# A MetaFormer block on one core: the last quarter of the convolution in two parts, the gate's chunks between their steps, five row buffers in place of three

## The chip, the cores and the metric

The kernel runs on one NeuronCore of a Trainium2 chip. Its engines are TensorE (PE in the profile, with PEld for its weight loads), VectorE (DVE), ScalarE (ACT) and GpSimd (POOL); SyncE (SP) issues nearly all plain DMAs, and GpSimd issues the indirect ones. The engines run their own instruction streams and wait for one another through semaphores. The metric is the device time of one execution, in microseconds.

## The reference, cut to what matters

`x` is 16 images of 64 channels and 56 x 56 pixels, in float32. Two blocks are computed, one after the other:

```
v = ln_over_channels(x)
r = relu(batchnorm(w1 @ v + b1))                    # 16 channels
ker = w2 @ r + b2                                   # 7 x 7 taps for each of 16 groups, at each pixel
x = x + sum over taps of shifted v * ker            # "involution": 16 groups of 4 channels
t = tokens of x (50176 of 64)
g = ln(t) @ Wg + bg;  top 2 of 8 experts, softmax over the two
t = t + sum over the two experts of weight * (gelu(ln(t) @ W1 + b1) @ W2 + b2)
```

All of it is kept to float32 accuracy.

## The kernel before, in words

Four stages follow one another, with a barrier of all engines between two: `norm_stage`, `conv_gate_stage`, `expert_stage`, `merge_stage`. The change lies in `conv_gate_stage`, and in `pieces` (line 693), which says where the pixels of a chunk lie in the images and which all later stages use.

**The convolution.** The images are taken in two parities of 8 images, and the rows of an image in two halves of 28. That gives four quarters (`QUARTERS`, line 79), and each quarter has a step for each of the 16 groups: 64 steps `t`. A step works on three strips of rows (`STRIP_SETS`, line 78). The first strip holds two blocks of 7 output rows, the other two strips one block each. For a strip, SP loads `xq` (112 or 119 partitions of 8 KB, lines 880 and 883), and once a step a `band` of filter weights (line 867). The first strip of a step, and the band, are split into a high and a low part: ACT writes the high parts (`split_band` line 959, `split_maps` line 965), DVE subtracts for the low ones (`low_parts`, line 1124). PE then needs three fast matmuls per product for that strip (lines 1054 to 1056). The other two strips are multiplied in plain float32 (line 1060), where one matmul is two instructions in the profile.

The products come in 8 units a step (`UNITS_OF`, line 86), 2 products of 119 x 448 each: units 0 to 3 for the split strip, 4 and 5, 6 and 7 for the others. Each goes to one of three PSUM buffers `z_ps`. DVE multiplies a unit by the reduced maps `r_all` (`weigh`, line 1135) into `prod`, and PE adds the blocks' taps up into `o_ps` (`sums`, line 1063). The sums of strips 0 and 1 stand after units 5 and 7 of the same step; those of strip 2 stand after unit 1 of the next step. Then ACT copies `o_ps` to `ob` (`evacuate`, line 979, first in ACT's work of a step) and SP stores it in eight DMAs (`store`, line 886).

**The order on each engine** is written out by hand. In step `t`, SP loads band and maps of `t`, then stores step `t-2`, then loads a chunk (lines 920 to 931); `store` waits for the evacuation, and all loads behind it in the queue wait with it. ACT evacuates `t-1`, splits band and maps of `t+1`, then does its share of the gate (line 1015). DVE does `low_parts(t+1)` after unit 3. PE's first unit of a step waits for both low parts (line 1039).

**The gate.** The 50176 tokens are 56 chunks of 896, 14 a quarter; a chunk can be worked on when its quarter's convolution has been stored. `load_chunk` (line 908) brings x and the convolution for it, in two DMAs for each image the chunk touches. PE's `unit` (line 1079) makes the centred rows and the raw gate scores, ACT takes them out of `u_ps` (`take_unit`, line 984), DVE adds up the squares (`variance`). Two chunks are a batch. ACT's `deviation` and DVE's `scores`, `first_choice`, `second_choice`, `number_duo` rank a batch in one step ("the rank step"); in the next ("the place step") DVE scans the batch, PE counts over the partitions (`counts`, line 1093), DVE fills the rows (`fill_rows`) and finds their places (`places`), and then POOL scatters the batch's rows to DRAM in 14 indirect DMAs (line 950). Rows and indices have three buffers (`RR`, line 711). `step_of` (line 845) puts chunk `c` of a quarter beside step `c + 2` of the next quarter. The last quarter has no next one: its 14 chunks are run in steps 66 to 79, with no convolution beside them.

After the last batch DVE works out a table of tiles (lines 1297 to 1364), SP stores it and writes 28 blank tiles at addresses that it reads from SBUF (line 938), and the stage ends when all of this and POOL's rows have landed.

**Later stages.** In `expert_stage` SP also loads x and the convolution chunk by chunk (`load_base`, line 1447); in `merge_stage` it stores each pair of chunks, one DMA for each image that a chunk touches (line 1679).

## Time and profile before

| | us |
|---|---|
| median of 3 runs | 2650.18 (2648.71 to 2662.69) |
| the profiled execution | 2656.94 |
| its span, first to last instruction | 2655.0 |
| granted TensorE clock, mean | 0.868 |
| PE busy, 10208 matmuls | 2018.9 (76%) |
| DVE busy | 1501.6 (57%) |
| ACT busy | 851.4 (32%) |
| POOL busy | 932.1 (35%) |

A busy share is an average over stages: PE is at 8 or 9 tenths in the slices of the convolution and of the experts, and at 3 to 1 tenths in three slices in the middle. Of POOL's time, 407.6 us are the 392 indirect DMAs of the gate, each 1040 ns.

### The profile page before, as it was taken

The numbers are of one execution on the slowest core, as the hardware profiler recorded it, in microseconds if no ns is written. First come the engines' busy times: TensorE is split into PE (matmuls) and PEld (weight loads), VectorE is DVE, ScalarE is ACT, GpSimd is POOL, SyncE is SP. The second block draws the span as 40 slices with busy tenths as digits, with TensorE's granted clock in tenths as the row PEclk, the third lists the DMA queues.
The fourth block names the chain that finished last, engine by engine and source line by source line (L and its number), as shares of the span: only waits on it lengthen the run. The fifth ranks groups of instructions, "written<-read, shape, count | busy, mean of one in ns | idle before, by whom it ended". The sixth has DMA issues, their size and how long they took to land. (4 is left out here: it accounts for less than half of the span.)

```text
span 2655.0 us, 34527 instructions
## 1 busy us (share of the span) xinstructions
PE 2018.9 (76%) x10208; PEld 1217.5 (46%) x10208; DVE 1501.6 (57%) x2687; ACT 851.4 (32%) x1540; POOL 932.1 (35%) x977
## 2 busy tenths in 40 slices
PE   5975889989889989898888321388787778778845
PEld 3742444445454445454444321255455555445533
DVE  2433566658778678786777534145444444444423
ACT  2431111122231222222322211255455555555510
POOL 5000000002433232430442566156555555555520
PEclk9977999999899999899999555689889899998965
DMA  8677777777877777777774320576666676766548
GB/s 238 143 155 172 181 190 188 184 188 204 203 187 186 194 193 194 195 180 199 195 202 102 86 63 32 153 211 199 188 198 197 195 199 196 200 191 201 165 123 274
DMA packets 291480, 474.17 MB, mean 179 GB/s; under 512 B 120156, under 2 KB 196059, under 8 KB 268327
## 3 DMA queue, kind: packets, MB, share of 16 engines
q1 hardware_dynamic: 260071, 441.41, 62.4%
q0 software_dynamic: 28832, 30.65, 4.1%
q8 instruction: 79, 1.29, 0.2%
q14 instruction: 98, 0.80, 0.1%
q10 hardware_dynamic: 2400, 0.01, 0.1%
HBM read 392.67 MB, written 81.93 MB: 179 GB/s over the span
## 5 line engine op out<-in xcount | busy, mean ns | idle before, releaser
L950 POOL DMA_INDIRECT token_rows<-gate_rows,gate_index x392 | 407.6, 1040 | 1039.1 <-DVE gate_index L1263 926.3
L1475 POOL DMA_INDIRECT mixed<-exp_mix,exp_xt x474 | 483.0, 1019 | 415.8 <-DVE exp_mix L1613 276.4
L1143 DVE TENSOR_TENSOR prod<-z_ps,r_all 119x896 f32<-119x896 f32 x512 | 543.2, 1084 | 130.3 <-PE z_ps L1056 79.5
L1060 PE MATMUL z_ps<-xq,band 112*119 112x448 f32 x1024 | 462.6, 588 | 123.3 <-DVE prod L1143 62.9
L1542 PE MATMUL exp_h_ps<-exp_tok,exp_pack 128*128 128x384 f32 x1264 | 292.2, 377 | 133.1 <-DVE exp_tok L1592 111.8
L1498 ACT ACTIVATE exp_hid<-exp_h_ps,exp_pack 128x384 f32<-128x384 f32 x632 | 341.3, 578 | 113.2 <-remote 67.1
L1060 PEld LDWEIGHTS z_ps<-xq,band 112*119 112x119 f32 x1024 | 185.9, 192 | 343.0 <-issue 259.6
L1542 PEld LDWEIGHTS exp_h_ps<-exp_tok,exp_pack 128*128 128x128 f32 x1264 | 234.2, 205 | 236.7 <-DVE exp_tok L1592 148.1
L1592 DVE CAST exp_tok<-exp_x_ps 128x384 fp32r<-128x384 f32 x158 | 88.1, 558 | 370.5 <-remote 216.8
L1554 PE MATMUL exp_y_ps<-exp_hid,exp_pack 128*64 128x384 f32 x1264 | 258.0, 532 | 0.0
L1073 PE MATMUL o_ps<-prod,pick 119*32 119x448 f32 x2048 | 254.2, 592 | 0.7 <-DVE prod L1143 0.3
L982 ACT ACTIVATE ob<-o_ps 128x448 f32<-128x448 f32 x64 | 34.8, 544 | 623.8 <-PE o_ps L1073 597.7
L1054 PE MATMUL z_ps<-xq_hi,band_hi 119*119 119x448 f32 x512 | 204.5, 399 | 25.9 <-DVE xq_lo L1132 18.0
L1055 PE MATMUL z_ps<-xq_lo,band_hi 119*119 119x448 f32 x512 | 187.6, 366 | 0.5 <-issue 0.5
L1056 PE MATMUL z_ps<-xq_hi,band_lo 119*119 119x448 f32 x512 | 187.2, 366 | 0.0
L1132 DVE TENSOR_TENSOR xq_lo<-xq,xq_hi 119x2048 fp32r<-119x2048 f32 x64 | 146.5, 2289 | 70.3 <-ACT xq_hi L970 69.1
L1505 ACT ACTIVATE exp_ysb<-exp_y_ps,exp_pack 64x384 f32<-64x384 f32 x158 | 90.9, 575 | 281.2 <-remote 135.2
L1088 PE MATMUL u_ps<-moe_gate_rhs,gate_xc 128*128 128x72 f32 x784 | 115.8, 309 | 73.8 <-issue 71.7
L970 ACT ACTIVATE xq_hi<-xq 119x2048 fp32r<-119x2048 f32 x64 | 122.2, 1909 | 137.7 <-DMA xq<-xs 132.1
L1054 PEld LDWEIGHTS z_ps<-xq_hi,band_hi 119*119 119x119 f32 x512 | 92.9, 182 | 133.3 <-issue 113.1
L1088 PEld LDWEIGHTS u_ps<-moe_gate_rhs,gate_xc 128*128 128x128 f32 x784 | 115.1, 226 | 77.3 <-issue 75.8
L1527 PE MATMUL exp_x_ps<-ident,exp_pair 128*128 128x128 f32 x474 | 88.0, 300 | 73.0 <-DVE exp_pair L1585 73.0
(194 smaller groups left out, 2119.6 us busy)
## 6 DMA issues: line engine op xcount, KB each, us to landing
xq<-xs SPq DMA_DIRECT2D x192, 896.0 KB
exp_pack<-packs SPq DMA_DIRECT2D x316, 321.5 KB
exp_xt<-token_rows SPq DMA_DIRECT2D x158, 120.0 KB
xs<-xpad SPq DMA_DIRECT2D x32, 448.0 KB, 5.7
xin<-in_x_dram SPq DMA_DIRECT2D x8, 1568.0 KB, 11.2
co<-ob SPq DMA_DIRECT2D x512, 24.5 KB
merge_yt<-mixed SPq DMA_DIRECT2D x28, 448.0 KB, 4.9
mixed<-exp_mix,exp_xt POOLq DMA_INDIRECT x474
```

Of the source, the lines that this page charges most:

```text
L950: pool.indirect_dma_start(out=token_rows[:, :], out_offset=bass.IndirectOffsetOnAxis(ap=index[b % RR][:, j:j + 1], axis=0), in_=rows[b % R ...
L1054: nc.tensor.matmul(zt, hi, maps[0], start=True, stop=False)
L1055: nc.tensor.matmul(zt, hi, maps[1], start=False, stop=False)
L1056: mm = nc.tensor.matmul(zt, lo, maps[0], start=False, stop=True)
L1060: mm = nc.tensor.matmul(zt, band[t % BR][rows_in, at:at + MF], maps, start=True, stop=True)
L1073: mm = nc.tensor.matmul(o_ps[32 * q:32 * (q + 1), 0:CN], pick[:, cols], prod[(NU * t + u) % PR][:, lot, :], start=i == 0 and lot == 0, sto ...
L1088: mm = nc.tensor.matmul(u_ps[:, GATE_COLS * j:GATE_COLS * (j + 1)], xc[n % XC][:, P * j:P * (j + 1)], tab.gate_rhs[:, :], start=True, stop ...
L1143: nc.vector.tensor_tensor(prod[(NU * t + u) % PR][:, :, :].rearrange("p m (d x) -> p m d x", d=D), z_ps[(NU * t + u) % 3][0:MF, :, 0:CN].r ...
L1475: pool.indirect_dma_start(out=mixed[:, :], out_offset=bass.IndirectOffsetOnAxis(ap=xt[t % XT][:, j, ROW_ID:ROW_ID + 1].bitcast(U32), axis= ...
L1498: nc.scalar.activation(hid[n % 8][:, :], h_ps[n % HT][:, 0:N], ACT.Gelu, bias=pack[t % WT][:, e, PACK_B1 + blk:PACK_B1 + blk + 1]).then_in ...
L1542: mm = nc.tensor.matmul(h_ps[n % HT][:, 0:N], pack[t % WT][:, e, cols].bitcast(F32R), tok[t % 2][:, :], start=not last, stop=last)
L1554: mm = nc.tensor.matmul(y_ps[t % 2][C * e:C * (e + 1), 0:N], pack[t % WT][:, e, at:at + C], hid[(t * 4 + BLK * e + blk) % 8][:, :], start= ...
```

## The change

- The last quarter (odd images, rows 28 to 55) is now two parts. The first is rows 42 to 55 of those images: 16 steps with the split strip alone. The second is rows 28 to 41: 16 steps with the two unsplit strips alone. The stage has 80 steps, the last 32 with 4 units each and 14 rows of output.
- Each of the two parts has 7 chunks, of 896 tokens as before; an image now gives 784 tokens to a part, so that every one of these 14 chunks touches two images.
- The chunks of the third quarter are put beside every second step of the first part (7 of them, steps 50 to 62), and beside the first 7 steps of the second part (64 to 70). The chunks of the first part are put beside the next 7 steps (71 to 77). Those of the second part stand behind the convolution (82 to 88).
- In the last 16 steps nothing is split: ACT and DVE have no high and low parts to make, and PE waits for the loads themselves.
- A loop of 8 slots remains in PE and DVE; a step of 4 units uses every second slot. The sums of a strip follow after the second unit that comes behind it.
- `RR` is 5 in place of 3.

The core of the diff:

```diff
-STRIP_SETS = ((0, 1, 2), (5, 4, 3))
-QUARTERS = ((0, 0), (0, 1), (1, 0), (1, 1))
+PARTS = ((0, 28, 0, (0, 1, 2)), (0, 28, 1, (0, 1, 2)), (28, 28, 0, (5, 4, 3)),
+         (42, 14, 1, (5,)), (28, 14, 1, (4, 3)))
+PART_CHUNKS = [height * W * P8 // CHUNK for _, height, _, _ in PARTS]
+CHUNK_STEPS = ([G + 2 + c for c in range(14)], [2 * G + 2 + c for c in range(14)],
+               [3 * G + 2 + 2 * c for c in range(7)] + [4 * G + c for c in range(7)],
+               [4 * G + 7 + c for c in range(7)], [5 * G + 2 + c for c in range(7)])
...
-    XR, PR, BR, XC, SQ, RR = 8, 6, 3, 3, 2, 3
+    XR, PR, BR, XC, SQ, RR = 8, 6, 3, 3, 2, 5
...
         def step_of(n):
-            return G * (n // QUARTER_CHUNKS + 1) + 2 + n % QUARTER_CHUNKS
+            k, c = part_of(n)
+            return CHUNK_STEPS[k][c]
...
+        SLOTS = len(UNITS_OF[0])
+        def unit_at(t, u):
+            if t >= STEPS:
+                return None
+            each = SLOTS // len(UNITS_OF[t // G])
+            return unit_no[t, u // each] if u % each == 0 else None
...
-                if t + 1 < STEPS:
+                if t + 1 < SPLIT_STEPS:
                     split_band(t + 1)
                     split_maps(t + 1)
...
-                if u == 0:
+                if split and u == 0:
                     pe.wait_ge(b_lo, t + 1)
                     pe.wait_ge(x_lo, t + 1)
-                elif u == LAST_UNIT[0] + 1 or u == LAST_UNIT[1] + 1:
-                    pe.wait_ge(x_in[n % XR], raw_uses(n % XR, n))
+                elif not split and (u == 0 or UNITS_OF[t // G][u - 1][0] != i):
+                    pe.wait_ge(band_in[t % BR], (t // BR + 1) * 16)
+                    pe.wait_ge(x_in[n % XR], raw_uses(n))
...
             for t in range(LAST):
-                for u in range(NU):
-                    if t < STEPS:
-                        filters(t, u)
-                    if u == 1 and 1 <= t <= STEPS:
-                        sums(t - 1, 2)
+                for u in range(SLOTS):
+                    v = unit_at(t, u)
+                    if v is not None:
+                        filters(v)
+                        for at in sums_after.get(v, ()):
+                            sums(*at)
                     if u == 2 and t in chunk_at:
                         unit(chunk_at[t])
-                    if u == 5 and t < STEPS:
-                        sums(t, 0)
                     if u == 6 and t in place_at:
                         counts(place_at[t])
-                    if u == 7 and t < STEPS:
-                        sums(t, 1)
...
-                    if u == 3 and t + 1 < STEPS:
+                    if u == 3 and t + 1 < SPLIT_STEPS:
                         low_parts(t + 1)
```

## Rows read from the trace of the kernel before

**Rows 1.** Stretches: length, busy per engine (instructions), granted clock, DMA share, GB/s.
```profile
1143.64:1455.95 312.31, 278.16 (x1364) 149.70 (x1364) 239.57 (x415) 77.09 (x117) 103.89 (x98) 0.95 0.68 177
1455.95:1655.90 199.95, 53.64 (x228) 50.30 (x228) 92.81 (x329) 40.48 (x75) 125.14 (x126) 0.51 0.21 61
```

**Rows 2.** Timeline of ACT, two steps: start, duration, line, operation, [idle before].
```profile
1377.35 0.55 ACT L982 ACTIVATE ob<-o_ps 128x448 f32<-128x448 f32 x1 [12.88 <-PE o_ps L1073]
...
1379.42 1.91 ACT L970 ACTIVATE xq_hi<-xq 119x2048 fp32r<-119x2048 f32 x1 [1.24 <-DMA xq<-xs]
1381.35 1.28 ACT L1003 ACT_TABLE_LOAD   x1
1382.64 0.31 ACT L1003 ACTIVATE gate_std<-gate_var,gate_eps_t 128x14 f32<-128x14 f32 x1
...
1402.42 0.55 ACT L982 ACTIVATE ob<-o_ps 128x448 f32<-128x448 f32 x1 [8.87 <-PE o_ps L1073]
...
1403.16 1.90 ACT L970 ACTIVATE xq_hi<-xq 119x2048 fp32r<-119x2048 f32 x1
...
1419.31 0.54 ACT L982 ACTIVATE ob<-o_ps 128x448 f32<-128x448 f32 x1 [12.89 <-PE o_ps L1073]
```

**Rows 3.** Timeline of ACT, the last evacuation of the convolution.
```profile
1455.94 0.54 ACT L982 ACTIVATE ob<-o_ps 128x448 f32<-128x448 f32 x1 [10.64 <-PE o_ps L1073]
```

**Rows 4.** Timeline of DVE in the same two steps.
```profile
1384.07 2.09 DVE L1143 TENSOR_TENSOR prod<-z_ps,r_all 119x896 f32<-119x896 f32 x2
...
1407.91 2.29 DVE L1132 TENSOR_TENSOR xq_lo<-xq,xq_hi 119x2048 fp32r<-119x2048 f32 x1
...
1411.11 0.17 DVE L1233 SCALAR_TENSOR_TENSOR gate_lean<-gate_side,gate_tanh 128x14 f32<-128x14 f32 x1
...
1412.42 2.08 DVE L1143 TENSOR_TENSOR prod<-z_ps,r_all 119x896 f32<-119x896 f32 x2
```

**Rows 5.** Groups by line, last quarter: busy, mean ns, idle before.
```profile
L1143 DVE TENSOR_TENSOR prod<-z_ps,r_all 119x896 f32<-119x896 f32 x128 | 135.5, 1083 | 23.5 <-PE z_ps L1060 7.4 <-PE z_ps L1056 6.7 <-remote 6.0
```

**Rows 6.** Timeline of PE in the same two steps.
```profile
1377.21 0.46 PE L1054 MATMUL z_ps<-xq_hi,band_hi 119*119 119x448 f32 x1
...
1378.52 1.68 PE L1088 MATMUL u_ps<-moe_gate_rhs,gate_xc 128*128 128x72 f32 x14
...
1406.39 3.17 PE L1060 MATMUL z_ps<-xq,band 112*119 112x448 f32 x8
1409.49 1.73 PE L1073 MATMUL o_ps<-prod,pick 119*32 119x448 f32 x16
```

**Rows 7.** Timeline of PE, a restart after an idle stretch.
```profile
905.08 1.67 PE L1060 MATMUL z_ps<-xq,band 112*119 112x448 f32 x4
911.34 3.34 PE L1060 MATMUL z_ps<-xq,band 112*119 112x448 f32 x4 [4.58 <-DVE prod L1143]
```

**Rows 8.** Timeline of SP's queue, one step: stores, chunk, band, maps.
```profile
1361.07 3.39 SPq L893 DMA_DIRECT2D co<-ob  x8
1364.50 0.51 SPq L916 DMA_DIRECT2D gate_xc<-in_x_dram  x1
...
1367.03 0.67 SPq L867 DMA_DIRECT2D band<-vf  x1
1367.75 1.01 SPq L880 DMA_DIRECT2D xq<-xs  x1
```

**Rows 9.** Timeline of PE behind the convolution, four of its chunks.
```profile
1466.63 3.23 PE L1088 MATMUL u_ps<-moe_gate_rhs,gate_xc 128*128 128x72 f32 x14 [0.65 <-issue]
...
1497.38 3.23 PE L1088 MATMUL u_ps<-moe_gate_rhs,gate_xc 128*128 128x72 f32 x14 [19.24 <-issue]
1501.84 3.24 PE L1088 MATMUL u_ps<-moe_gate_rhs,gate_xc 128*128 128x72 f32 x14 [1.22 <-issue]
...
1520.21 3.24 PE L1088 MATMUL u_ps<-moe_gate_rhs,gate_xc 128*128 128x72 f32 x14 [1.42 <-issue]
```

**Rows 10.** Timeline of POOL behind the convolution, single scatters [idle before].
```profile
1510.79 1.02 POOL L950 DMA_INDIRECT token_rows<-gate_rows,gate_index  x1 [17.32 <-DVE gate_index L1263]
...
1546.55 0.97 POOL L950 DMA_INDIRECT token_rows<-gate_rows,gate_index  x1 [0.31 <-issue]
1556.02 1.02 POOL L950 DMA_INDIRECT token_rows<-gate_rows,gate_index  x1 [8.50 <-DVE gate_index L1263]
```

**Rows 11.** Timeline of ACT behind the convolution, one chunk taken.
```profile
1540.01 0.54 ACT L990 ACTIVATE gate_rows<-u_ps 128x448 f32<-128x448 f32 x1 [20.14 <-issue]
```

**Rows 12.** Timeline of POOL and SP's queue, POOL's last scatter and the blank tiles.
```profile
1654.63 0.97 POOL L950 DMA_INDIRECT token_rows<-gate_rows,gate_index  x1 [0.30 <-issue]
...
1659.88 26.57 SPq L938 DMA_DIRECT2D token_rows<-moe_blank  x25
```

More of the change, by code:

```diff
@@ L88 @@
              for i, r in enumerate(strips) for q in range(0, CH, 3 - len(STRIP_BLOCKS[r]))]
-            for strips in STRIP_SETS]
-NU = len(UNITS_OF[0])
-LAST_UNIT = [max(u for u, (i, _) in enumerate(UNITS_OF[0]) if i == k) for k in range(len(STRIP_SETS[0]))]
+            for _, _, _, strips in PARTS]
 XS_H = C * P8 * WP
@@ L690, in _, with part_of @@
             dve.wait_ge(bn_own, 11)
+def part_of(n):
+    k = max(k for k in range(len(PARTS)) if FIRST_CHUNK[k] <= n)
+    return k, n - FIRST_CHUNK[k]
 def pieces(n):
-    quarter, c = divmod(n, QUARTER_CHUNKS)
-    s, par = QUARTERS[quarter]
+    k, c = part_of(n)
+    top, height, par, _ = PARTS[k]
+    per_image = height * W
     at, end = c * CHUNK, (c + 1) * CHUNK
@@ L699, in pieces @@
     while at < end:
-        i, pos = at // HALF, at % HALF
-        size = min(end - at, HALF - pos)
-        runs.append((PARITY * i + par, HALF * s + pos, at - c * CHUNK, size))
+        i, pos = at // per_image, at % per_image
+        size = min(end - at, per_image - pos)
+        runs.append((PARITY * i + par, top * W + pos, at - c * CHUNK, size))
         at += size
@@ L845, in step_of @@
         def step_of(n):
[L846 removed]
+            k, c = part_of(n)
+            return CHUNK_STEPS[k][c]
         def placing_step(b):
@@ L914, in load_chunk @@
                 for img, at, to, size in pieces(n):
-                    for lot, part in enumerate((x, co)):
+                    for lot, maps in enumerate((x, co)):
                         sp.dma_start(xc[n % XC][C * lot:C * (lot + 1), to:to + size],
-                                     part[img].rearrange("c h w -> c (h w)")[:, at:at + size]
+                                     maps[img].rearrange("c h w -> c (h w)")[:, at:at + size]
                                      ).then_inc(xc_in[n % XC], 16)
@@ L922, in _ @@
                     load_band(t)
-                    for i in range(GS):
+                    for i in range(len(part(t)[3])):
                         load_maps(t, i)
-                        for part in range(len(R_PARTS)):
-                            if R_STEPS[part] == t and i == min(part, 1):
-                                load_r(part)
+                        for lot in range(len(R_PARTS)):
+                            if R_STEPS[lot] == t and i == min(lot, 1):
+                                load_r(lot)
                 if 0 <= t - 2 < STEPS:
@@ L1063, in sums @@
             def sums(t, i):
-                pe.wait_ge(weighted, NU * t + LAST_UNIT[i] + 1)
+                last = len(part(t)[3]) - 1
+                blocks = [m for r in part(t)[3] for m in STRIP_BLOCKS[r]]
+                pe.wait_ge(weighted, strip_end[t, i])
                 if i == 0 and t >= 1:
                     pe.wait_ge(ob_done, t)
-                for u, (kind, parts) in enumerate(UNITS_OF[quarter_of(t)[0]]):
+                for u, (kind, parts) in enumerate(UNITS_OF[t // G]):
                     if kind != i:
@@ L1273, in _ @@
                 if t in R_NEED:
-                    dve.wait_ge(r_ready, max(part for part in range(len(R_PARTS)) if R_NEED[part] == t) + 1)
-                for u in range(NU):
-                    if t < STEPS:
-                        weigh(t, u)
+                    dve.wait_ge(r_ready, max(lot for lot in range(len(R_PARTS)) if R_NEED[lot] == t) + 1)
+                for u in range(SLOTS):
+                    if unit_at(t, u) is not None:
+                        weigh(unit_at(t, u))
                     if u == 1 and t in rank_at:
```

164 lines of the change are left out of this document (93 added, 71 removed).

## The prediction

> **What bounds the kernel now.** I read the page first: its 40 slices show PE at 8 or 9 tenths in the convolution and in the experts, and a trough between them. The stretches give it a size [rows 1]: the last quarter takes 312.3 us from the evacuation before it to the last one, with PE 89% and DVE 77% busy. Behind it lie 199.95 us until POOL's last scatter, with PE 27% busy at half clock and DMA at 0.21. This second stretch is what the change shortens, by running 7 of its 14 chunks beside the convolution. It can pay for that only in the first.
>
> Next the timeline of a pair of steps in the convolution [rows 2]. Evacuations stand at 1377.35, 1402.42 and 1419.31: a rank step of 25.1 us and a place step of 16.9 us, seven of each in a quarter. The place step is full: the reader can add PE's work [rows 6], where four split units are 4 x 1.31, the other two strips 2 x 3.17, the sums 2 x 1.7 and the chunk 1.5: 16.5 us. The rank step is long because DVE waits for the deviation, which ACT makes only after it has split the next step's maps, here 1.24 us late for their DMA. PE then runs dry, and a restart shows what that costs beyond the wait [rows 7]: the same four instructions take 1.67 us before 4.58 us of idle time and 3.34 after it. That is TensorE at 1.2 GHz where it had been at 2.4.
>
> Last the tail. A chunk that meets no obstacle follows the one before after 4.46 us, 1497.38 to 1501.84 [rows 9]. But POOL needs about 18 us for a batch: 14 scatters of 0.97 us with 0.30 between them are 17.8, and two batches back to back took 36.7, 1510.79 to 1547.5 [rows 10]. While it works off two batches the other engines slow down: PE begins the chunk at 1520.21, 3.24 us of work by its records, and ACT gets it at 1540.01 [rows 9, 11]. SP writes only 3 of its 28 blank tiles until POOL has stopped, then 25 in 26.6 us [rows 12]. I do not know why; that it goes with POOL's runs is what the rows show.
>
> **The first part: 16 steps with the split strip alone.** The work would fit into 7 us: PE has 4 x 1.31 + 1.7 = 6.9 us, DVE four products and the low parts, 4 x 1.05 + 2.6 = 6.8 [rows 4 to 6]. What sets the step is a chain that a long step hides behind its other strips. From the evacuation of t-1: ACT's copy, band and maps, 2.64 us (1402.42 to 1405.06); DVE's low part, 2.29; PE's first two units of t+1, 2.62, and the sums of t, 1.73, which release the next evacuation. With hand-overs that is 9.35 us [rows 2, 4, 6]. PE is then idle at least 2.4 us a step, so part of it runs at 1.2 GHz; nothing gives +0, all of PE's share twice as long gives +4.35. I take +2, since the slow stretch is one of a few us [rows 7]. That makes 11.3 us.
>
> The loads are a second chain. The maps of t+1 stand in SP's queue behind the store of t-2, which waits for an evacuation, and on even steps behind a chunk. The maps are issued 6.7 us after the stores begin with a chunk and 4.2 without [rows 8]. They landed 11.7 us later at the latest (1367.75 to 1379.42), with three strips a step in the queues; here there is one, and I take 6.5. So on even steps the split can begin 0.6 + 6.7 + 6.5 = 13.8 us after the evacuation one step earlier, and two steps take 13.8 + 8.6 + 2 = 24.4 us. Seven such pairs are 171 us, two steps without chunks 22.6. Three rank steps add 1.6 for table and deviation, 1.1 for the scores and a product ahead of the low parts, 3.9 each; three place steps add `fill_rows`, 1.3 to 1.5 [rows 2, 4]. The sum is 210 us. Its ends are 166 (the bare chain) and 235 (all at 1.2 GHz, no more DMA waits).
>
> **The second part: 16 steps with the two unsplit strips.** PE has 6.3 + 1.7 + 1.5 + 0.2 = 9.7 us where there is a chunk [rows 6]. DVE has 4.2 for the products; the gate costs it (239.57 - 135.5 - 15 x 2.7) / 14 = 4.5 us a chunk, together 8.8 [rows 1, 4, 5]. The DMA engines are busy 0.68 of 19.5 us now [rows 1]; with two strips of three, half the stores and a chunk a step I estimate 9.5 to 10. Three resources near 10 us do not interlock without loss. The rank step no longer waits for a split, so I take 11.4 for 14 steps and 18.6 for the two without a chunk: 178 us, between 153 and 216. SP has 3.4 + 2.5 + 0.7 + 1.7 = 8.3 us of issuing a step, which fits, though it is close.
>
> The quarter thus goes from 312.3 to 388 us, **+76**; both parts at their ends would give +7 and +139.
>
> **The tail.** Before, POOL's last row begins 198.7 us after the last evacuation, at 1654.63, and ends at 1655.6: E + 199.7 [rows 3, 12]. After it: the first chunk at E + 10.7 as now (1455.94 to 1466.63), the third 2 x 4.46 later; it stands in the step that places batch 24, and POOL starts 8.95 us after such a chunk (1501.84 to 1510.79), at E + 28.6. Two batches and the idle time behind them take 45.2 us (1510.79 to 1556.02), since the chunks stall as now; the last two batches, at 18.1 each between the two figures above, end at E + 28.6 + 45.2 + 36.2 = E + 110. **-90**. Without idle time between batches it is E + 101 (-99); with the 17.3 us of idle time before one batch [rows 10], and one more such gap, -73. What follows POOL's last row, mostly the 25 blank tiles, stays.
>
> **At nothing.** Five row buffers: when ACT took the chunk at 1540.01, POOL's batch in that slot, the first of the pair, had ended at about 1528.9, so three did not hold it. I cost them at 0, with up to -9 if the idle time of 8.5 us were theirs. Two more memsets lie ahead of the first loads' landing: 0 to 2 us. Chunks that touch two images bring 8 more DMAs in each loop: in the experts SP has room, in the merge stage up to 0.6 each; I take +1, bounds 0 and +6.
>
> Sum: 76 - 90 + 1 = -13, with rounding -14. The profiled execution, 2656.9 us, would be 2643; it lies 6.8 above the median of the runs, so the median comes to **2636 us**.
>
> **Rivals.** (1) *TensorE stays at 1.2 GHz all through the first part.* For it: every step leaves PE idle behind its burst, and the clock has fallen after such a gap [rows 7]. Then a step without chunk takes 5.0 + 8.7 = 13.7 us; with one, PE's own work of 3 + 5.2 delays it to about 16: with the 16 us for rank and place steps that is 9 x 13.7 + 7 x 16 + 16 = 251 us, 41 more than my 210: 2677 us, slower. It decides once PE's share of the chain runs at half clock in every step, and not only in its first units. Against it: gaps in the trace are followed by only a few slow us. The Trainium skill, "TensorE: Matmul & The Clock Gate", section "HAM oscillation — how this bites in real kernels", states this rule: where each burst is shorter than the wait before it, every burst starts cold. The trace agrees for one burst [rows 7]; by that rule the sum is this rival's, by the short slow stretch it is mine.
>
> (2) *The chains overlap better.* Maps land sooner and the clock holds: first part 185, second 170, and the tail's batches follow without idle time: 43 - 99 + 1 = -55, 2595 us. For it: the DMA queues have a third of the strips. Against it: the chain of 9.35 us is in the order of the program.
>
> (3) *POOL's runs meet.* In the second part a batch is due every 22.8 us and takes 18. If DVE places one late and the next early, PE stalls as at 1520.21, 16.6 us a time (1523.4 to 1540.0). Two such stalls are +33 on the convolution; POOL is then further along at its end, which I value at 10: 2659 us. Against it: a gap of nearly 5 us is left.
>
> **Chances.** Forecast 0.42 (its own range 2618 to 2654), rival 1 0.20, rival 2 0.20, rival 3 0.18. A median within 0.5%, 2637 to 2663, could hardly be told from no change. Faster than that: 0.24 of the forecast and 0.18 of rival 2. Within: 0.18, 0.02, 0.06 of rival 1 and 0.10 of rival 3. Slower: 0.14 and 0.08. The range, 2600 to 2680, holds the forecast and rivals 1 and 3, and leaves out the half of rival 2 below its value and the ends of the bounds.
>
> **What would show it.** Evacuations in steps 48 to 63 about 12 us apart (near 9 speaks for rival 2, 14 for rival 1, with the granted clock between 0.5 and 0.6); in steps 64 to 79 about 11.4. ACT's `split_maps` idle for DMA on even steps. POOL's last row 105 to 115 us after the last evacuation; no pair of batches back to back before step 79. I am wrong if the quarter grows by less than 40 us or more than 110, or if the tail shrinks by less than 75.

## The result and the profile after

The changed kernel takes **2711.52 us** (median of 4 runs, 2702.95 to 2714.6) against 2649.44 us of the kernel before beside it: a ratio of **1.0224, 95% interval 1.0191 to 1.0258**. It is slower by some 60 us; the prediction had 2636 us, and its range ended at 2680. The profiled execution took 2714.6 us, its span is 2712.8 us (57.8 more than before), the granted clock 0.854.

The three stretches that answer to [rows 1], in the same columns: first part, second part, and the last evacuation to POOL's last row.

```profile
1138.01:1374.68 236.67, 153.42 (x767) 105.29 (x768) 147.96 (x243) 60.86 (x84) 69.98 (x66) 0.80 0.43 111
1374.68:1614.30 239.62, 185.96 (x713) 83.59 (x711) 138.74 (x321) 44.76 (x86) 93.57 (x97) 0.83 0.64 167
1614.30:1723.10 108.80, 26.83 (x114) 25.14 (x114) 47.41 (x179) 20.53 (x38) 61.71 (x62) 0.50 0.22 66
```

| us | before | predicted | after |
|---|---|---|---|
| start to evacuation 47 | 1143.6 | same | 1138.0 |
| first part, steps 48 to 63 | - | 210 | 236.7 |
| second part, steps 64 to 79 | - | 178 | 239.6 |
| the quarter | 312.3 | 388 | 476.3 |
| last evacuation to POOL's last row | 199.7 | 110 | 108.8 |
| the rest | 999.4 | +1 | 989.7 |

So the span's +57.8 us is +164.0 in the quarter, -90.9 in the tail, -5.6 and -9.7 in stretches that the change hardly touches. The tail came out as forecast. These are ScalarE's last evacuation and POOL's batches behind it (as [rows 3, 10, 12]):

```profile
1614.30 0.55 ACT L1023 ACTIVATE ob<-o_ps 128x448 f32<-128x448 f32 x1 [7.05 <-remote]
```

```profile
1641.74 1.02 POOL L990 DMA_INDIRECT token_rows<-gate_rows,gate_index  x1 [20.50 <-DVE gate_index L1311]
...
1686.84 1.01 POOL L990 DMA_INDIRECT token_rows<-gate_rows,gate_index  x1 [8.63 <-DVE gate_index L1311]
...
1722.16 0.97 POOL L990 DMA_INDIRECT token_rows<-gate_rows,gate_index  x1 [0.30 <-issue]
```

The batches go in pairs as before, with 8.6 us idle between the two pairs, and end 108.8 us after the last evacuation. The whole error lies in the convolution: PE is busy 0.65 and 0.78 of the two parts, where it was busy 0.89 of the quarter [rows 1].

**A pair of steps in the first part.** ScalarE, as [rows 2]:

```profile
1261.68 0.55 ACT L1023 ACTIVATE ob<-o_ps 128x448 f32<-128x448 f32 x1 [10.38 <-PE o_ps L1119]
...
1271.16 0.55 ACT L1023 ACTIVATE ob<-o_ps 128x448 f32<-128x448 f32 x1 [3.99 <-PE o_ps L1119]
1274.14 0.40 ACT L1003 ACTIVATE band_hi<-band 119x238 fp32r<-119x238 f32 x1 [2.43 <-DMA band<-vf]
1276.67 1.91 ACT L1011 ACTIVATE xq_hi<-xq 119x2048 fp32r<-119x2048 f32 x1 [2.13 <-DMA xq<-xs]
1278.60 1.28 ACT L1044 ACT_TABLE_LOAD   x1
1279.89 0.31 ACT L1044 ACTIVATE gate_std<-gate_var,gate_eps_t 128x14 f32<-128x14 f32 x1
...
1291.96 0.55 ACT L1023 ACTIVATE ob<-o_ps 128x448 f32<-128x448 f32 x1 [3.87 <-PE o_ps L1119]
```

SP's queue of the same pair, as [rows 8], and VectorE and PE:

```profile
1262.25 3.35 SPq L932 DMA_DIRECT2D co<-ob  x8
1265.70 0.65 SPq L906 DMA_DIRECT2D band<-vf  x1
1266.39 1.00 SPq L919 DMA_DIRECT2D xq<-xs  x1
```

```profile
1282.63 2.28 DVE L1179 TENSOR_TENSOR xq_lo<-xq,xq_hi 119x2048 fp32r<-119x2048 f32 x1
1285.01 0.70 PE L1098 MATMUL z_ps<-xq_hi,band_hi 119*119 119x448 f32 x1 [11.33 <-DVE xq_lo L1179]
```

The reader can follow one chain: evacuation at 1261.68, stores from 1262.25, band at 1265.70 and maps at 1266.39, ScalarE idle for them until 1276.67, the split, the deviation's table ahead of VectorE's low part at 1282.63, PE at 1285.01, evacuation at 1291.96. Two steps in 30.3 us. The granted clock of these two steps, as windows:

```profile
1271.16:1291.96 20.80, 9.47 (x42) 6.27 (x42) 11.25 (x27) 5.95 (x7) 0.00 (x0) 0.67 0.36 90
1291.96:1302.12 10.16, 8.89 (x59) 6.77 (x60) 9.73 (x19) 3.62 (x6) 0.00 (x0) 1.00 0.42 108
```

The long step's 0.67 is a mean over two levels. PE has nothing to do from 1273.7 to 1285.01; the granted clock is full until 1276.91, 0.50 (1.2 GHz) until 1290.57, and full again behind that. A matmul of the first burst takes 0.57 us there, in place of 0.36. The short step has the full clock throughout.

The same wait stands in six of the 16 steps. In the steps of ScalarE behind evacuations 49, 51, 54, 56, 58 and 60 the split of the maps begins 5.5 to 6.8 us after the evacuation; where the loads are there it begins 0.73 us after it. In all six it begins 10.2 to 11.6 us after the issue of the maps. In four of them, this pair among them, no chunk stands before the band in SP's queue.

**A step of the second part.** ScalarE's evacuations, and VectorE around the second one:

```profile
1481.07 0.55 ACT L1023 ACTIVATE ob<-o_ps 128x448 f32<-128x448 f32 x1 [9.86 <-PE o_ps L1119]
...
1500.44 0.55 ACT L1023 ACTIVATE ob<-o_ps 128x448 f32<-128x448 f32 x1 [11.83 <-remote]
```

```profile
1491.57 0.17 DVE L1261 SCALAR_TENSOR_TENSOR gate_duo<-gate_tri,gate_lower 128x14 f32<-128x14 f32 x1
1500.29 1.09 DVE L1191 TENSOR_TENSOR prod<-z_ps,r_all 119x896 f32<-119x896 f32 x1 [8.55 <-remote]
```

Steps alternate there, 10 to 14 us and 16 to 20, where 11.4 was forecast. In the long ones lies one of POOL's batches, here 1480.19 to 1497.7, and the engines' waits carry the releaser "remote". That drew me to POOL first. It was a wrong lead for most of the loss.

### The profile page after: what moved, and what is told of

The parts are those of the page before. It is cut to its first block and busy times, and to the rows that moved or that the text cites. A ratio compares the mean times of both kernels' runs of the same rounds, so it can differ in the third digit from the quotient of the medians.

```text
span 2712.8 us, 34775 instructions
## 1 busy us (share of the span) xinstructions
PE 2056.4 (76%) x10208; PEld 1238.8 (46%) x10208; DVE 1506.0 (56%) x2687; ACT 861.8 (32%) x1556; POOL 930.4 (34%) x979
## 5 line engine op out<-in xcount | busy, mean ns | idle before, releaser
L1104 PE MATMUL z_ps<-xq,band 112*119 112x448 f32 x1024 | 480.2, 608 | 128.5 <-issue 65.0
L1546 ACT ACTIVATE exp_hid<-exp_h_ps,exp_pack 128x384 f32<-128x384 f32 x632 | 343.0, 580 | 110.6 <-remote 57.3
L1104 PEld LDWEIGHTS z_ps<-xq,band 112*119 112x119 f32 x1024 | 193.7, 200 | 356.2 <-issue 271.9
L1098 PE MATMUL z_ps<-xq_hi,band_hi 119*119 119x448 f32 x512 | 213.1, 416 | 101.8 <-DVE xq_lo L1179 53.6
L1023 ACT ACTIVATE ob<-o_ps 128x448 f32<-128x448 f32 x80 | 43.6, 546 | 732.2 <-PE o_ps L1119 644.7
L1099 PE MATMUL z_ps<-xq_lo,band_hi 119*119 119x448 f32 x512 | 197.1, 385 | 0.0
L1100 PE MATMUL z_ps<-xq_hi,band_lo 119*119 119x448 f32 x512 | 196.2, 383 | 0.0
L1098 PEld LDWEIGHTS z_ps<-xq_hi,band_hi 119*119 119x119 f32 x512 | 99.0, 193 | 199.5 <-issue 175.6
L1119 PEld LDWEIGHTS o_ps<-prod,pick 119*32 119x32 f32 x2048 | 53.7, 116 | 174.1 <-issue 136.4
L1134 PE MATMUL u_ps<-moe_gate_rhs,gate_xc 128*128 128x72 f32 x784 | 110.0, 299 | 27.9 <-issue 13.7
## 6 DMA issues: line engine op xcount, KB each, us to landing
xin<-in_x_dram SPq DMA_DIRECT2D x8, 1568.0 KB, 11.1
band<-vf SPq DMA_DIRECT2D x80, 110.6 KB
```

The source lines that it names most:

```text
L1098: nc.tensor.matmul(zt, hi, maps[0], start=True, stop=False)
L1099: nc.tensor.matmul(zt, hi, maps[1], start=False, stop=False)
L1100: mm = nc.tensor.matmul(zt, lo, maps[0], start=False, stop=True)
L1104: mm = nc.tensor.matmul(zt, band[t % BR][rows_in, at:at + MF], maps, start=True, stop=True)
L1119: mm = nc.tensor.matmul(o_ps[32 * q:32 * (q + 1), 0:CN], pick[:, cols], prod[unit_no[t, u] % PR][:, lot, :], start=m == blocks[0], stop=m ...
L1546: nc.scalar.activation(hid[n % 8][:, :], h_ps[n % HT][:, 0:N], ACT.Gelu, bias=pack[t % WT][:, e, PACK_B1 + blk:PACK_B1 + blk + 1]).then_in ...
```

## The experiments

Kernels named a_ are edits of the changed kernel, those named b_ of the kernel before. Chips differ, so whole times are compared only as a ratio to runs of the kernel before on the same chip. The convolution is compared by its stretches, in one profiled execution each: from evacuation 47 to 63 and from there to 79. The first three quarters took 888 to 907 us in all of them. That does not make a stretch of the last two parts free of the chip: the first part with loads two steps early took 197.0 to 198.9 us in four kernels on one chip and 183.6 to 187.2 us in three kernels on another, though in its code only the output and row buffers and the spread of POOL's scatters differ between them. So a difference of the first part across chips can be off by some 15 us.

| kernel | first part | second part | ratio to before [95%] |
|---|---|---|---|
| changed | 236.7 | 239.6 | 1.0224 [1.0191, 1.0258] |
| scatters spread (`a_pace`) | 233.6 | 231.7 | 1.0143 [1.0085, 1.0201] |
| scatters in halves (`a_halves`) | 228.6 | 229.7 | 1.0142 [1.0084, 1.0199] |
| loads 1 step early (`a_lead`) | 199.5 | 234.2 | 1.0067 [1.0044, 1.0089] |
| loads 2 steps early (`a_deep`) | 197.0 | 232.1 | 1.0165 [1.0120, 1.0209] |
| + spread (`a_deep_pace`) | 198.8 | 225.0 | 1.0106 [1.0060, 1.0152] |
| + chunks early (`a_chunk_deep_pace`) | 198.9 | 212.0 | 1.0067 [1.0037, 1.0098] |
| same, not spread (`a_chunk_deep`) | 197.1 | 236.2 | 1.0134 [1.0064, 1.0204] |
| + first chunk too (`a_best`) | 183.6 | 214.4 | 1.0186 [1.0162, 1.0210] |
| + four output buffers (`a_ring`) | 187.2 | 207.2 | 1.0176 [1.0146, 1.0206] |
| same, not spread (`a_ring_runs`) | 185.7 | 208.8 | 1.0160 [1.0134, 1.0187] |
| `a_ring` + stores from ScalarE (`a_two_queues`) | 206.4 | 197.1 | 0.9982 [0.9960, 1.0005] |
| no gate work in the last parts (`a_nogate`) | 212.4 | 198.9 | 1.0849 [1.0776, 1.0922] |
| same, loads early (`a_deep_nogate`) | 168.7 | 181.2 | 1.0760 [1.0716, 1.0804] |
| same, four output buffers (`a_ring_nogate`) | 168.9 | 174.5 | 1.0715 [1.0684, 1.0747] |

Undivided: before 312.3; loads early (`b_lead`) 305.1, 0.9978 [0.9947, 1.0010]; spread (`b_pace`) 312.0, 0.9996 [0.9968, 1.0024]; five row buffers (`b_rr5`) 311.5, 1.0003 [0.9978, 1.0029]; no gate work (`b_nogate`) 268.0, 1.0366 [1.0334, 1.0398].

`a_best`, `a_ring`, `a_ring_runs`, `a_ring_nogate`, `a_deep_nogate` and `b_nogate` ran on one chip, on which the kernel before takes 2420 us; the last section says what is different there. `a_pace`, `a_halves`, `a_lead` and `a_nogate` ran on a second chip (before: 2689 us). `a_deep`, `a_deep_pace`, both `a_chunk_deep` kernels, `a_two_queues`, `b_lead`, `b_pace` and `b_rr5` ran on a third (2653, and 2684 at the time of `a_two_queues`).

### POOL's scatters spread, or cut in halves

```diff
  pool.wait_ge(placed, b + 1)
+ t = placing_step(b)
+ first, last = (min(step_end[min(k, STEPS - 1)], len(units)) for k in (t, t + 2))
  for j in range(BB):
+     if last > first:
+         pool.wait_ge(z_done, first + (last - first) * j // BB)
```

In halves: `if j == BB // 2: pool.wait_ge(ob_done, min(placing_step(b) + 2, STEPS))`.

> The changed kernel, but POOL's 14 scatters of a batch are spread over the two steps behind the placing, one for every 14th part of these steps' units, in place of one unbroken run of 17.5 us. Theory A (a long unbroken run of scatters on POOL stalls the other engines from some 12 us on until it ends; in the changed kernel VectorE waits 8.55 us at 1500.29 and ScalarE 11.83 us at 1500.44, and POOL's run ends at 1497.7): the seven steps of the second part in which a run falls shrink from 18.5 to 20.3 us to 12 to 14, the second part from 239.6 us to 185 to 200, the first part by 0 to 15 us, the whole by 45 to 90 us. Theory B (these steps are long because a batch's gate work is in them, ranking on VectorE, tables on ScalarE, the chunk's 14 matmuls that wait for a DMA): the second part stays at 235 to 245 us. Theory C (TensorE's granted clock, 0.83 in the second part, sets it): no change either.

> The changed kernel, but POOL waits in the middle of a batch for the evacuation two steps behind the placing, so that a run has 7 scatters (some 8.7 us) in place of 14. Theory A, if the stall comes only after some 12 us of a run: gone as with the even spread, second part 185 to 200 us. If it comes from the number of scatters whatever their spread: as before the edit. Theory B and C: 235 to 245 us.

> The kernel before with POOL's scatters of a batch spread over the two steps behind the placing. Its steps alternate between 16.9 and 20 to 25 us, and POOL's run of 18.5 to 19 us lies in the longer ones. Theory A: the longer steps shrink by 2 to 4 us each, over 21 batches placed in the convolution 40 to 80 us of the whole, and the last quarter falls from 312.3 us to 285 to 300. Theory B (the longer steps are the ranking's work): quarter within 6 us, the whole within 0.5%.

The second part became 7.9 and 9.9 us shorter, not 40 to 55. With the spread its first eight steps became even, 14 to 16 us, and their pairs stayed near 30. In the kernel before the spread gave nothing. Theory A is not the cause of most of the loss.

### Loads ahead of the stores

In the changed kernel's last two parts SP now goes through `loads(t + 1)`, `store(t - 2)`, `load_chunk` in that order, where it had `store(t - 2)`, `load_chunk`, `loads(t + 1)`; in `b_lead` through the whole convolution.

> The changed kernel, but in the last two parts SP issues the band and maps of a step before the stores of the step three before it, not behind them. Theory D (the first part's pairs of 27 to 31 us are one chain: evacuation at 1261.68, eight stores until 1265.60, band issued at 1265.70 and landed at 1274.14, maps at 1276.67, split, low part, TensorE again at 1285.01): each pair loses the 3.4 us of the stores and a part of the landing, 4 to 8 us, so the first part shrinks from 236.7 us to 180 to 210, and the second part by 0 to 15. Rival (the landing of the loads comes late by what else the DMA engines carry, or ScalarE and VectorE set the pair): within 8 us of 236.7.

> The kernel before (undivided last quarter), but SP issues the loads of each step ahead of the stores of the step three before it, through the whole convolution. Theory G (in full steps of 16.9 us and more the chain of loads has slack; it becomes the bound only where steps are half as long): the last quarter stays within 6 us of 312.3 and the whole within 0.5% of the kernel before. Rival (the chain is late in full steps too): the last quarter falls by 15 us or more and the whole by 30 or more.

```profile
1146.90:1346.41 199.51, 142.35 (x754) 98.30 (x755) 147.18 (x243) 59.61 (x84) 73.42 (x64) 0.86 0.51 135
1346.41:1580.57 234.16, 185.93 (x726) 90.05 (x725) 138.87 (x321) 45.02 (x86) 96.78 (x100) 0.83 0.64 166
```

Theory D holds: the first part becomes 37.2 us shorter by an edit that moves nothing but the loads in SP's queue (29.1 and 34.1 us against the two kernels above, on the same chip). ScalarE no longer waits for a load in any of its steps. In full steps the same edit gives 7.2 us of the quarter, a little over the 6 expected, and the whole is the same. The second part did not answer, 5.4 us.

### Loads two steps early

```diff
- XR, PR, BR, XC, SQ, RR = 8, 6, 3, 3, 2, 5
+ XR, PR, BR, XC, SQ, RR = 8, 6, 4, 3, 2, 4
```

and `loads(t + 2)` where the kernel above has `loads(t + 1)`.

> The changed kernel, but SP issues the loads of the last two parts' steps two steps earlier than it does now and ahead of the stores (band buffers 4 in place of 3, for which the gate's row buffers go from 5 to 4). Theory E (the second part's 15 us a step is a chain over three steps: evacuation at 1448.43, eight stores and two chunk loads until 1453.5, band and two maps issued until 1460.8, landed some 10 us later, then the step's units; moving only the stores left it at 234.2 us since SP waits for the band buffer): the first part takes 190 to 205 us, as with the loads one step earlier (199.5), and the second part falls from 239.6 us to 185 to 210. Theory A (POOL's runs stall the others): the second part stays above 225 us, with the steps of POOL's runs at 19 to 21 us. Theory F (TensorE's own work at the granted clock, 185.9 us busy of 239.6, and what moves over the DMA engines at 167 GB/s are the bound): above 225 us, with steps that are even.

> The kernel with the loads two steps earlier, and POOL's scatters spread over two steps as well. The spread alone brought the second part from 239.6 us to 231.7 only: it made the steps even (14 to 16 us, before 10 to 14 and 18 to 20), and their pair stayed at 30 us. If the chain of loads had hidden what the spread gives (Theory A beside E), the second part comes out 20 to 50 us under the same kernel without the spread; if the stall in POOL's runs only takes up time in which the chain waits anyway, within 8 us of it.

Theory E is refuted for the second part with its gate work: 232.1 us. With the spread it is 225.0, a gain of 7.1 us, just inside "within 8". But PE's waits in that run named the next thing that is late:

```profile
PE u_ps L1143 <- DMA gate_xc<-co: 40.8, 14, 6.0
```

The gate's unit stands at the third unit slot of the very step in which SP issues its chunk. PE waited for all 14 chunks of the part.

### The division without gate work

Chunks of the last two parts' (or the last quarter's) steps are moved behind the convolution:

```diff
-                [3 * G + 2 + 2 * c for c in range(7)] + [4 * G + c for c in range(7)],
-                [4 * G + 7 + c for c in range(7)], [5 * G + 2 + c for c in range(7)])
+                [5 * G + 2 + c for c in range(14)],
+                [5 * G + 16 + c for c in range(7)], [5 * G + 23 + c for c in range(7)])
```

> The changed kernel with all 28 chunks of the last three parts behind the convolution, so that no gate work stands in its last 32 steps. It gives the price of the division alone. If the divided convolution itself is as the prediction took it (11.3 us for a step of the first part and some 8 of the second), the two parts take 180 and 125 us, together within 10 us of the undivided last quarter of the kernel before (312.3 us with its gate work). If the division itself is the loss (chain of loads, half the columns' work for the same instructions), the first part stays at 225 us or more without any gate work.

> The kernel before with the last two quarters' 28 chunks behind the convolution: its undivided last quarter without gate work. With the divided one (212.4 and 198.9 us without gate work, 411.3 in all) it gives the price of the division alone. The first quarter, which has no gate work either, takes 14.9 to 17 us in most steps, so 250 to 270 us are expected, and a price of 140 to 160 us for the division; the prediction had 76 us for division and its gate work together. If it takes 290 us or more, the gate work is nearly free in full steps and the division costs 120 or less.

> The changed kernel with no gate work in the last two parts and the loads two steps earlier. Theory E (the division's own price is the lateness of the loads): the first part falls from 212.4 us to 160 to 180 and the second from 198.9 to 140 to 165. Theory F (TensorE's and VectorE's own work, or the DMA engines' rate): together not under 380 us.

Windows of the two parts as changed, of the undivided quarter, and of the two parts with loads two steps early:

```profile
1149.72:1362.13 212.41, 139.88 (x641) 94.36 (x642) 117.88 (x131) 44.95 (x51) 30.28 (x28) 0.79 0.37 95
1362.13:1560.98 198.85, 149.25 (x504) 55.11 (x504) 67.66 (x62) 8.71 (x17) 0.00 (x0) 0.88 0.60 155
```

```profile
1139.18:1407.20 268.02, 247.47 (x1144) 123.76 (x1144) 181.51 (x193) 45.19 (x50) 30.20 (x28) 0.97 0.68 171
```

```profile
1145.21:1313.88 168.67, 126.95 (x641) 85.80 (x642) 116.74 (x131) 43.17 (x50) 31.26 (x28) 0.89 0.52 133
1313.88:1495.11 181.23, 143.16 (x504) 52.73 (x504) 67.69 (x62) 8.69 (x17) 0.00 (x0) 0.91 0.57 150
```

This is the main reading. The divided parts take 411.3 us and the undivided quarter 268.0 with no chunk beside them: division alone costs **143.3**. The expectation of `a_nogate` had set 225 us or more in the first part for this cause, and it is 212.4; it is the sum of both parts, 99 us over the 312.3 of the quarter with its gate work, that rules out the prediction's step lengths (180 and 125). The gate adds 44.3 us for 14 chunks undivided (312.3 - 268.0) and 65.0 for 21 divided (476.3 - 411.3): 3.2 and 3.1 us a chunk, the same. So only the seven chunks brought in, some 22 us, are the gate's; the rest of the 164 is the division's own.

`a_nogate` and `b_nogate` ran on different chips, and so did `a_nogate` and `a_deep_nogate`. By the 15 us above, I estimate that the 143 is right to about that much. Early loads give back 61.4 us of it, 43.7 in the first part and 17.6 in the second, of which up to 15 in the first part can be the chip. What no chip blurs is the price with loads early: 349.9 against 268.0 us, 81.9, both on one chip. The second part stayed 16 us short of the expected 140 to 165. ScalarE's waits there name what comes late next:

```profile
ACT ob L1028 <- DMA co<-ob: 154.9, 13, 12.6
```

The evacuation waits for the stores of the output buffer two steps back.

### Chunks one step early, with and without the spread

From step 65 on SP issues `load_chunk(chunk_at[t + 1])` first in step `t`, ahead of band and maps.

> The kernel with loads two steps earlier and POOL's scatters spread, and from step 65 on SP issues the load of a gate chunk one step ahead of its unit and ahead of the maps, not in the unit's own step. Theory H (a unit of 14 gate matmuls stands at the third unit slot of the very step in which its chunk is issued; a half step leaves half the time for it: in the kernel without this edit TensorE waits 40.8 us for the chunk's DMA, in 14 of 16 steps, 4.46 us at 1497.14): that wait goes to under 8 us and the second part falls from 225.0 us to 180 to 200, the whole by 25 to 45 us, about to the kernel before. Theory F (TensorE at its granted clock, 181.6 us busy of 225.0, and the DMA engines' rate are the bound): the wait moves to the maps or the step's matmuls, and the second part stays above 215.

> The same, but POOL's 14 scatters of a batch in one run as in the changed kernel. It prices POOL's runs where loads and chunks come early. Theory A as a second limit beneath the loads: the second part is 20 to 45 us longer than with the spread, with the steps of the runs at 18 to 20 us. If the stall in POOL's runs was only the chunk's late DMA read under another name: within 8 us of the kernel with the spread.

13.0 us less with the spread, at 212.0; the range was 180 to 200. One step of 27.6 us holds a wait of 21.4 us for the one chunk that the edit left late, the first of the fourth part. Without the spread the part is 24.2 us longer on the same chip, and the median of the whole 18.9 us: here POOL's runs do cost something. As changed the spread gave 7.9 us, and with loads but not chunks early 7.1; I read this as the late chunk covering the rest.

### The rest of the rings, and a second queue

`a_best` takes the first chunk early too. `a_ring` has `ob` and `ob_out` with four buffers (`ob[t % 4]`, rows `RR` 3). In `a_two_queues` ScalarE issues the stores of the last two parts behind its work of a step:

```diff
                 if t in rank_at:
                     lean_to(rank_at[t])
+                if 3 * G <= t - 1 < STEPS:
+                    store(act, t - 1)
```

> The kernel with loads two steps early, chunks one step early and the scatters spread, and now the first chunk of the fourth part early too. In the run without this edit that one step took 27.6 us, in which TensorE waited 21.4 us for the chunk. Expected: that step at 10 to 15 us, the second part at 190 to 202 us (212.0), the whole 10 to 20 us less, within 0.5% of the kernel before. If the wait moves on (maps late in the steps behind): the second part stays above 206.

> The kernel with loads two steps early, chunks one step early and the scatters spread, and four output buffers in place of two (the gate's row buffers go from 4 to 3). In the run with two, ScalarE waits 83.1 us in 8 steps for the stores of the buffer two steps back, which stand behind 1.8 MB of maps in the queue. Theory K (a ring of n buffers is n steps of time, and half steps halve it): the wait goes, the second part falls from 214 us to 170 to 190, the whole to 0.2 to 1.5% under the same kernel with two buffers' ratio of 1.0186, that is 0.998 to 1.010 of the kernel before. Theory F' (the DMA engines cannot carry the second part's 174 GB/s much faster): the wait moves to the maps or the chunk and the part stays above 205.

> The kernel with loads two steps early and no gate work in the last two parts, with four output buffers. It gives the division's own price once no ring is late: undivided 268.0 us, divided 411.3 as changed, 349.9 with early loads. Theory K: the second part falls from 181.2 us to 140 to 155, the first stays within 5 us of 168.7, so that 40 to 60 us of the division's 143 are left, the engines' own share. Theory F': the second part stays above 172.

> The same with POOL's 14 scatters in one run. With the loads early but two output buffers the runs cost 24.2 us of the second part (236.2 against 212.0). Theory A: 20 to 45 us longer than with the spread. If that difference was chance: within 8 us.

> The kernel with four output buffers, and in the last two parts the eight stores of a step are issued by ScalarE behind its work of the step, on a queue of its own, not by SP. Theory L (SP's issuing is the bound: 4.0 us of stores, 2.5 of chunk loads, 0.7 of band, 8 of maps in a row): a cycle of SP falls from 15.5 us to 11 to 12, the steps of the second part to 11 to 13 us, the part from 207 us to 172 to 190; the first part, where VectorE and ScalarE set the pace, stays within 8 us of 187. Theory F (the DMA engines' rate): SP's issue of the maps takes as much longer as the stores took, and the part stays above 200. Rival on ScalarE: the 4 us of issuing make its table loads and the deviation late, and the first part grows by 10 us or more.

`a_best`: the step of 27.6 us is gone, but the part stayed at 214.4 where 190 to 202 was expected, in steps of about 15 us. `a_ring` missed its 170 to 190 too. Its second part has five steps of 10.2 us in a row, and then steps of 11 to 17: the loads that lay ahead are used up. Without gate work it is the same, steps of 8.1 to 8.2 us four times, and then pairs of 24 to 27, and the part stays above the 172 us of Theory F':

```profile
1310.74:1485.28 174.54, 141.37 (x504) 52.65 (x504) 67.68 (x62) 8.69 (x16) 0.00 (x0) 0.90 0.59 155
```

Theory K is right for a few steps and wrong for the part: two more output buffers gave 7.2 us with gate work and 6.7 without. `a_ring_runs`, without the spread, took 208.8 us, 1.6 more, where Theory A had 20 to 45. SP's queue of `a_ring` in two later steps shows what is left:

```profile
1454.90 4.01 SPq L932 DMA_DIRECT2D co<-ob  x8
1458.96 0.51 SPq L956 DMA_DIRECT2D gate_xc<-in_x_dram  x1
...
1461.49 0.70 SPq L906 DMA_DIRECT2D band<-vf  x1
1462.23 8.56 SPq L919 DMA_DIRECT2D xq<-xs  x2
1470.83 4.03 SPq L932 DMA_DIRECT2D co<-ob  x8
...
1478.16 7.57 SPq L919 DMA_DIRECT2D xq<-xs  x2
1485.78 0.58 SPq L932 DMA_DIRECT2D co<-ob  x1
```

There is no gap in it: stores 4.0, chunk 2.5, band 0.7, maps 7.6 to 8.6 us, 15 to 16 us in all, and that is the step. Without the stores on it, on ScalarE's queue, the same stretch of `a_two_queues` reads:

```profile
1463.67 11.63 SPq L930 DMA_DIRECT2D xq<-xs  x2
1475.35 0.59 SPq L956 DMA_DIRECT2D gate_xc<-in_x_dram  x1
...
1479.12 11.12 SPq L930 DMA_DIRECT2D xq<-xs  x2
```

```profile
1150.87:1357.30 206.43, 148.73 (x753) 100.41 (x753) 147.40 (x243) 59.44 (x83) 72.44 (x64) 0.84 0.54 139
1357.30:1554.37 197.07, 170.04 (x728) 79.59 (x726) 138.30 (x321) 44.89 (x86) 95.58 (x98) 0.90 0.71 184
```

The stores are gone from SP's queue and its cycle is as long as before, 15.5 us (1463.67 to 1479.12): the issue of the maps takes 11.1 to 11.6 us. Over the seven cycles of SP from the band of step 71 to that of step 78 one takes 15.4 us on average in `a_ring` and 14.7 here, and the maps' issue 7.9 and 11.1. So of the 4.0 us that the stores left free, 3.2 went into the maps' issue. Theory L, that SP's own issuing is the bound, fails by this: what was taken off the queue came back in the maps' issue. This is the rival's sign, though the part came out just under its 200, at 197.1; `a_ring` ran on another chip, and 6.4 of the 10.1 us between them lie in the part's first step (19.3 and 12.9 us).

What the queue waits for is not shown. The two kernels move 189 and 196 GB/s over these seven cycles, and the undivided convolution before moves 192 (300 to 1143 us of its trace), which speaks for the transfers' rate as the limit. But in `a_ring_nogate` SP stands 7.0 to 8.6 us in the maps' issue too, over the same seven cycles, at 164 GB/s.

The first part is 206.4 us: 7.6 more than `a_chunk_deep_pace` on the same chip (198.9), 19.3 more than `a_ring` on the other (187.2), which the expectation had named. By that number the rival on ScalarE came true; on the same chip it stays under its 10 us.

### Five row buffers

`RR` 5 in the kernel before.

> The kernel before with five row buffers in place of three, the one part of the change that stands by itself. As ScalarE's wait for a row buffer ends no wait of the trace in the convolution, the prediction put it at 0: the whole within 0.5% of the kernel before, each stage within 5 us. Rival (the buffers let ScalarE and VectorE run ahead in the tail, where POOL's runs merge): the tail of 199.7 us changes by more than 10 us.

1.0003, and every stretch within 4 us: 0, as forecast.

No kernel beats the one before by what can be measured. `a_two_queues` (0.9982) and `b_lead` (0.9978) equal it.

## Why the prediction was wrong, step by step

- **The tail, -90:** right, -90.9, by its own steps.
- **The chain that sets a step of the first part, 9.35 + 2:** right in size. With loads early and no gate work the steps alternate 11.0 and 9.5 us. With loads early and all gate work the part took 199.5 us (`a_lead`); the prediction's sum without waits for loads is 16 x 11.3 + 16 = 197. Rival 1, the half clock throughout, did not come true, though its time of 2677 us was nearest: the clock was 0.67 in the long step and 1.00 in the short one. For the rule of the Trainium skill's "TensorE: Matmul & The Clock Gate" that each burst starts cold, the trace agrees in every second step from 1233.72 on: a matmul takes 0.57 us behind 11.33 us of idle time, and the step behind it, with a chunk's matmuls ahead of its units, has no cold burst.
- **"Landed 11.7 us later at the latest ... I take 6.5":** failed. From the maps' issue at 1266.39 ScalarE waited until 1276.67, 10.3 us, and 10.2 to 11.6 us in all six steps that waited. I had taken fewer strips in the queues for a shorter landing; it is as long as before. The waits for loads cost 37.2 us (`a_lead`), where the prediction had 7 x (24.4 - 22.6) = 12.6. The chunk's 2.5 us ahead of the band, which the chain counted in every pair, were there in only two of the six steps, so a late pair came out 1.8 to 6.5 us over its forecast, and not 3.8 each time.
- The first two steps, without a chunk, took 31.0 us against 22.6. The first of them ranks the last batch of the quarter before: four steps of the part rank and four place, where the prediction counted three of each. That leaves 3 us of the 8.4 unexplained.
- The band is the smaller load of the two, 110.6 KB, and yet ScalarE got it only 8.4 us after its issue (1265.70 to 1274.14). The trace's packet records show most of that time: the load's 119 packets of 952 bytes go one behind the other, from 1267.1 to 1273.7, while of the maps' packets, 8192 bytes each, 7 are in flight at once on average. In the 16 steps of the part the last packet of a band ended 7.7 to 11.9 us after its issue. The Trainium skill, "DMA: Bandwidth & Descriptors", section "Why a DMA increments its semaphore by 16 and not by 1", says that a transfer runs on the largest number of engines, 16 at most, that divides the slowest dimension of both its sides. The band's are 17 rows and 119 partitions, so by that rule one engine carries it, and the trace agrees: one packet at a time. No run here changed the band's shape, so what that would give stays open.
- **"Three resources near 10 us ... 11.4 for 14 steps, 18.6 for the two":** failed, the largest error, 61.6 us. I added the engines' work and asked which is the longest. Without gate work the step takes 12.4 us (198.9 / 16), where my 18.6 for two had 9.3. That is 50 of the 61.6; the gate's 40.7 us for 14 chunks, for which I had 2.1 us each, are the other 11. What the sum left out is that each resource is reached through a ring whose depth is counted in steps, and half steps halve the time that a ring gives. The runs show this for a part of the 50 only: loads two steps early gave 17.6 us without gate work (measured across two chips), four output buffers 6.7 more, and 174.5 us is still 26 over 16 x 9.3. With gate work, all edits together brought the part from 239.6 to 197.1.
- **"SP has ... 8.3 us of issuing a step, which fits":** failed. I took the maps' issue, 1.7 us for two, from a stretch where the queue was short. In the second part of the changed kernel it is 1.6 to 9.5 us, and in `a_ring`, where loads are asked for without pause, 5.7 to 9.9; there SP's cycle is the step.
- **Rival 3, POOL's runs meet:** they did not meet, but long steps lay in POOL's runs. The price was 24.2 us with loads and chunks early, and some 8 as changed.
- **Five row buffers, memsets, eight more stores:** 0, shown for the buffers in the kernel before. What follows POOL's row came out 9.7 us shorter; it varied from 990 to 1021 us over kernels with the same code in it, so I read no effect there.
- **"Wrong if the quarter grows by more than 110":** it grew by 164.

What stays open is the rest of the division's price: 75.4 us without gate work when loads come early and the output ring is deeper (343.4 against 268.0, on the same chip). In the first part PE's, ScalarE's and VectorE's chain has no other strip to hide behind, by the prediction's own account; in the second the transfers were seen only through SP's issue times and the packets' rate, and the band, which has one packet in flight for 5.7 to 8.2 us of every step (`a_ring`), was left as it is.

## What to carry to other kernels

A ring of n buffers, or a load issued n positions ahead in a queue, is worth n steps of time. Halve the step and every one of them becomes half as early, even if each engine's work also halves; a load's landing does not halve with it. Before dividing a loop, go through the rings and in-order queues and ask for each: issue to landing, how many new steps is that? And when a wait is relieved, price the next one before counting the gain: here the order was loads, chunk, output buffers, the issuing queue.

## What the hardware showed that I had not expected

- **"Remote" waits and POOL's runs differ by chip.** The waits with the releaser "remote" add up to 581 us in the trace before and 584 after. On the chip of `a_best`, `a_ring`, `a_ring_runs` and of the kernels without gate work but `a_nogate`, the trace has none. There POOL's unbroken runs cost 1.6 us in the second part (208.8 against 207.2), on another chip 24.2; the output buffers differ between these two comparisons too, so the chip is a likely reason and not a shown one. And the kernel before takes 2420 us there against 2650 to 2690 elsewhere; the convolution's first three quarters are alike (888 to 902 us), and what lies behind POOL's last row takes 801 to 812 us instead of 990 to 1021. What these waits are no run shows. In the convolution they go with POOL's runs: 41 us in the trace before, none in that of `b_pace`, where the scatters are spread, and yet the quarter took the same time (312.3 and 312.0).
- **The issue of a DMA takes as long as the queue makes it.** Two maps of 896 KB each are issued in 1.7 us where the queue is short, in 7.9 on average over the seven cycles of `a_ring`, and in 11.1 over those of `a_two_queues`. Moving the stores to another engine's queue took 4.0 us of issuing off SP and shortened its cycle by 0.7.
- **A small load can land nearly as late as a large one.** The band's 119 packets went nearly always one at a time (1.02 to 1.11 in flight on average) and took 5.3 to 8.3 us in the traces before and after and in those of `a_ring`, `a_two_queues` and `b_nogate`, in full steps and in half ones.
